# One more head pair of the first layer masked inside VectorE's row maxima, and a new order of all operations of a three-layer decoder kernel

## The reference

```python
attn = einsum('bhqd,bhkd->bhqk', q, k) / sqrt(16)
attn = softmax(where(mask, attn, -inf))
z = einsum('bhqk,bhkd->bhqd', attn, v)
x = layernorm(x + z @ W_proj + b_proj)                      # layers 0 and 1
x = layernorm(x + z + einsum('bsef,bse->bsf', experts, combine))   # layer 2
```

## Time and profile before

| what | value |
|---|---|
| median of three executions | 892.4 us |
| profiled execution, its own time | 893.21 us |
| span of the profile (first to last instruction) | 891.4 us |
| mean granted TensorE clock | 0.993 of 2.4 GHz |
| PE busy | 866.1 us, 97% |
| DVE busy | 758.7 us, 85% |
| ACT busy | 585.7 us, 66% |
| POOL busy | 416.8 us, 47% |
| DMA queue q1 | 98.77 MB, 40.6% of 16 engines' span |

### The profile page before, as it was taken

The page is one execution under the profiler, slowest core; times in us unless marked ns, Lnnn a source line. Parts: engine busy times, 40 slices in busy tenths (PEclk is TensorE's granted clock), DMA queues, the critical chain, the costliest instruction groups (busy, mean ns, idle before and its releaser), DMA issues.

```text
span 891.4 us, 28532 instructions
## 1 busy us (share of the span) xinstructions
PE 866.1 (97%) x10018; PEld 746.3 (84%) x10018; DVE 758.7 (85%) x3509; ACT 585.7 (66%) x1211; POOL 416.8 (47%) x588
## 2 busy tenths in 40 slices
PE   7899999999999999999999999999999999999996
PEld 4788888888888888989888888888888888888874
DVE  4689988998988898888888988888888888888895
ACT  4688888788878787887877644444445554555533
POOL 7688887888864545354444421122222222222201
PEclk8999999999999999999999999999999999999998
DMA  5756655664545454444434222222333333323201
GB/s 183 206 158 167 178 146 156 169 176 131 165 119 144 121 147 131 115 128 113 129 98 121 79 57 60 68 67 72 85 85 85 85 85 85 85 73 84 74 25 61
DMA packets 98268, 100.58 MB, mean 113 GB/s; under 512 B 10704, under 2 KB 90704, under 8 KB 98128
## 3 DMA queue, kind: packets, MB, share of 16 engines
q1 hardware_dynamic: 98128, 98.77, 40.6%
HBM read 18.25 MB, written 4.19 MB: 25 GB/s over the span
## 4 chain that ended last, share of the span: by engine, by line
PE 78%; issue 8%; POOL 5%; ACT 4%; DVE 2%; DMA 2%; SPq 1%; ACTq 0%; POOLq 0%; DVEq 0%
PE work L512 42%; PE work L655 9%; PE max_scores L609 8%; PE scores L632 8%; PE work L664 4%; PE scores L635 3%; PE work L537 1%; ACT attn L815 1%; PE work L673 1%; POOL attn L1156 1%; DMA k_stack<-k_parts 1%; POOL k_parts L1105 1%; POOL rstd L1147 1%; POOL q_parts L1105 1%; DMA k_stack<-in_vo 1%
## 5 line engine op out<-in xcount | busy, mean ns | idle before, releaser
L815 ACT ACTIVATE attn<-scores 128x512 f32<-128x512 f32 x384 | 214.9, 600 | 124.0 <-PE scores L632 111.1
L982 DVE CUSTOM_DVE_ANT_0 max_scores<-max_scores,mask_qk 128x128 f32<-128x128 f32 x872 | 222.9, 325 | 30.3 <-PE max_scores L609 29.3
L1098 POOL TENSOR_TENSOR q_full<-q_full,q_parts 128x512 f32<-128x512 f32 x48 | 55.9, 1166 | 274.2 <-ACT q_parts L773 274.2
L609 PE MATMUL max_scores<-k_stack,q_stack 126*128 126x128 bf16 x1536 | 142.4, 220 | 2.7 <-DMA k_stack<-k_parts 1.6
L632 PE MATMUL scores<-q_stack,k_stack 128*128 128x128 bf16 x1536 | 137.1, 220 | 3.4 <-DMA q_stack<-neg_max_t 1.6
L1057 DVE SCALAR_TENSOR_TENSOR x_all<-work,combine,x_all 128x256 f32<-128x256 f32 x256 | 121.8, 481 | 18.0 <-PE work L512 13.4
L985 DVE TENSOR_REDUCE neg_max<-max_scores 128x4 f32<-128x512 f32 x166 | 111.0, 682 | 24.1 <-PE max_scores L609 16.2
L609 PEld LDWEIGHTS max_scores<-k_stack,q_stack 126*128 126x128 bf16 x1536 | 98.1, 97 | 33.0 <-issue 18.7
L982 DVE DVE_READ_ACCUMULATOR2_ANT neg_max<- 128x1 f32 x872 | 122.9, 141 | 0.0
L632 PEld LDWEIGHTS scores<-q_stack,k_stack 128*128 128x128 bf16 x1536 | 98.1, 97 | 26.4 <-ACT attn L815 8.1
L512 PE MATMUL work<-split_hi,w_hi 128*128 128x256 f32 x384 | 113.2, 295 | 3.2 <-DVE split_lo L884 3.2
(11 more groups left out here) (126 smaller groups left out, 2020.5 us busy)
## 6 DMA issues: line engine op xcount, KB each, us to landing
k_stack<-k_parts SPq DMA_DIRECT2D x288, 128.0 KB, 2.5
q_stack<-q_parts SPq DMA_DIRECT2D x288, 128.0 KB, 2.5
in_t<-in_xt SPq DMA_DIRECT2D x16, 256.0 KB, 3.0
x_all<-in_x SPq DMA_DIRECT2D x16, 256.0 KB, 3.2
in_t<-in_ct SPq DMA_DIRECT2D x16, 256.0 KB, 2.7
out<-x_all SPq DMA_DIRECT2D x16, 256.0 KB, 2.2
stage<-in_e SPq DMA_DIRECT2D x4, 512.0 KB, 4.6
stage<-in_qk SPq DMA_DIRECT2D x2, 512.0 KB, 5.0
```

Of the source, the lines that this page charges most:

```text
L609: mm = pe.matmul(dst[:, b, h2, :], head(QS, n, 2 * p + h2, b, ROWS), head(KS, n, 2 * p + h2, b, ROWS), start=(b + h2 == 0), stop=(b + h2 = ...
L815: act.activation(attn("exp", n, p)[:, :, :], SS[g % 2][:, :, :, :].rearrange("k b h q -> k (b h) q"), ACT.Exp).then_inc(probs_done, 1)
L982: ins = dve.tensor_tensor_reduce(scores, scores, MQ[l][:, :], -1.0, HUGE, ALU.add, ALU.min, NM[n % 2][:, b, h:h + 1])
L1098: pool.tensor_tensor(FULL[x][:, :, :], FULL[x][:, :, :], PART[x][:, 0, :, :], ALU.subtract).then_inc(rest_done[x], 1)
```

## The change

Pair 7 of layer 0 joins the pairs whose mask DVE adds. That concerns items 1 to 15: PE has 15 matmuls of 512 columns fewer (8453 instead of 8468 in the program), DVE has 60 add-and-reduce instructions, with their reads, in place of 15 reductions. Layer 1 had all 8 pairs in the list already.

`PERIOD`, `TIMES`, `SHIFTS`, `starts` and `base` go. In their place `ITEM_TIMES` holds a planned time for every operation of each of the 48 items, so every item has an order of its own. The times of the weight pieces and of the two bias rows are new as well. No other function changes; banks and buffers are handed out by the same rules from the new order. Line numbers after the change are 425 higher in the functions of the engines.

```diff
-MAX_DVE = ((0, 1, 2, 4, 5, 6), (0, 1, 2, 3, 4, 5, 6, 7))
+MAX_DVE = ((0, 1, 2, 4, 5, 6, 7), (0, 1, 2, 3, 4, 5, 6, 7))
...
-PERIOD = [16.65, 18.91, 28.45]
-
-TIMES = [
-    {"q": [-39.5], "qe": [-36.65], "qh": [-35.05], "qr": [-30.39], "qm": [-27.24], "ql": [-26.79], "qs": [-38.33,
...
-SHIFTS = {
...
+ITEM_TIMES = {
+    0: {"in": [-28.35], "xr": [28.72], "xh": [-3.83], "xl": [-61.07], "q": [-15.02], "qe": [-7.1], "qh": [2.19],
...
-BIAS_TIMES = [(-27.38, -57.89), (133.26, 140.23)]
...
+BIAS_TIMES = [(3.2, -5.21), (138.61, 144.42)]
...
-ORDER = sorted([(base(n) + t + SHIFTS.get(n, {}).get(kind, 0.0), kind, n, part) for n in range(NITEM)
-                for kind, times in TIMES[layer(n)].items() for part, t in enumerate(times)]
+ORDER = sorted([(t, kind, n, part) for n in range(NITEM) for kind, times in ITEM_TIMES[n].items() for part, t in enumerate(times)]
```

More of the change, by code:

```diff
@@ L60 @@
 RB_COLS = 2 * D + E
-PERIOD = [16.65, 18.91, 28.45]
-TIMES = [
[8 rows of a table removed]
-     "norm": [33.1], "causal": [3.14, 4.3, 5.5, 6.05, 7.5, 7.59, 9.11, 10.11], "va": [-16.07]},
[12 rows of a table removed]
-     -23.67, -19.94, -18.8, -15.5, -15.16, -10.78, -9.61], "max": [-23.51, -22.57, -19.37, -17.73, -14.15,
[3 rows of a table removed]
-     [-57.01], "xl": [-54.92], "gexp": [-27.59], "gtop": [-20.22], "gateT": [-18.57], "cbt": [-17.56], "bias":
[L93 to L96, removed]
@@ L109 @@
 }
 PIECES = ["qk1", "vo1", "qk2", "vg2", "e0", "e1", "e2", "e3"]
-PIECE_TIMES = [(-8.49, 40.1, 47.02), (43.97, 76.14, 80.28), (71.5, 90.0, 111.17), (112.45, 133.83, 143.74), (140.64, 174.8, 178.0), (177.55, 192.88, 213.63), (266.43, 287.47, 303.57), (323.0, 337.9, 343.55)]
-BIAS_TIMES = [(-27.38, -57.89), (133.26, 140.23)]
-def starts():
-    first = [0.0]
-    for l in range(1, NL):
-        end, gaps = first[-1] + PERIOD[l - 1] * (NSTEP - 1), [PERIOD[l - 1]]
-        for kind in TIMES[l]:
-            if kind in TIMES[l - 1]:
-                gaps.append(max(TIMES[l - 1][kind]) - min(TIMES[l][kind]) + 0.1)
-        first.append(end + max(gaps))
-    return first
@@ L132 @@
-FIRST_BASE = starts()
-def base(n):
-    l, p = divmod(n, NSTEP)
-    return FIRST_BASE[l] + p * PERIOD[l]
+PIECE_TIMES = [(45.15, 59.57, 64.45), (78.58, 94.06, 96.95), (104.81, 112.12, 121.58), (137.24, 150.69, 164.53), (164.97, 178.87, 179.5), (189.64, 196.1, 208.83), (267.09, 270.52, 284.33), (307.08, 311.22, 312.95)]
+BIAS_TIMES = [(3.2, -5.21), (138.61, 144.42)]
 def layer(n):
```

246 lines of the change are left out of this document (added), and 274 rows, old and new, of tables (ITEM_TIMES, SHIFTS, TIMES).

## The result

The changed kernel takes 909.4 us (median of 6 runs, 907.2 to 915.8) against 892.1 us (6 runs of the kernel before on the same chips): the ratio is 1.021, with a 95% interval from 1.019 to 1.023. It is slower by 17 us where 5.8 us less were forecast, and it lies outside the range. The profiled execution took 912.1 us, its span is 910.3 us (before: 893.2 and 891.4). Times of the experiments are medians of 4 to 12 executions; one execution, of `new_sp_by_ready`, took 2134.0 us where its other three took 914.0 to 915.3, the record has no cause for it, and the ratio leaves it out.

A forecast was written before the change was run, and what follows sets the result against it. PE was taken as the bound, 97% busy, with waits left in layer 0. Terms -3.3 - 4.9 + 1.5 + 0.8 - 1.4 + 1.5 = -5.8 us gave 886.6 us; forecast range 884.5 to 889.5, 8-in-10 range 881.5 to 893.

The forecast's parts named there:

- The mask on PE: Layer 0: PE loses a 0.22 us mask matmul in each of 15 items, counted whole, -3.3 us.
- the mask is not on the path: Rival, layer 0: the mask's 3.3 us returns as waits for `max`; -2.5 us, 889.9 us, chance 0.06.
- The mask on DVE: Layer 0: DVE gains 0.41 us an item, 6.2 us in 15, against 1.7 us idle an item.
- DVE as the bound of layer 0: Rival, layer 0: DVE's added 0.41 us lengthens each item; +7.1 us, 899.5 us; slower had chance 0.13.
- Fewer waits for `zt`: Layer 0: more PE work between `zT` 1 and `zt` cuts waits from 6.4 to 1.5 us, saving 4.9.
- The start: Item 0: `q` no longer covers `maxt`'s wait for the maxima; loss 0.8 us, bounds nothing to 1.4.
- The ends of the layers: Items 46 and 47: more PE work from `k` to `s1` 0 removes waits, -1.4 us, bounds 0 and 2.
- Layers 1 and 2 otherwise: Layers 1 and 2: tighter distances, such as bank reuse in layer 2, add 1.5 us, bounds nothing and 4.9.
- DVE's maxima come late next: Layer 0: DVE's maxima must come sooner and take back 0.1 us an item, +1.5 us; bounds nothing and 6.2.
- Layer 0's period: Sign to check, layer 0: the item's period falls from 14.4 to about 13.9 us.

The follow-up runs named there:

- new_sp_by_ready: The changed kernel with SP's list sorted by when each copy's data was ready in the changed kernel's trace; 915.0 us, ratio 1.025.
- mask_only: The kernel before in its old order, with pair 7 of layer 0 masked on DVE; 892.7 us, ratio 1.0003.
- old_v_late_mask: The kernel before with the mask on DVE and `v` of layer 0 moved from -18.37 to -17.7; 893.0 us, ratio 1.0011.
- order_only: The changed kernel with its new order, but pair 7 of layer 0 masked on PE as before; 907.8 us, ratio 1.019.
- the control: The kernel before without the low part of `q` and `k` and their copies from item 3 on; 890.8 us, ratio 0.9986.
- the copy that went aside: The changed kernel with low copies from item 3 on sent to an unread DRAM tensor, `s1` 0 not waiting for them; 894.5 us, ratio 1.0029.
- new_low_by_pool: The changed kernel with POOL instead of SP issuing the low copies, right behind `kl` and `ql`; 943.4 us, ratio 1.058.
- new_pe_2us_early: The changed kernel, banks chosen from profiled starts, with only PE's order taken from moving `q` and `k` up to 2 us earlier, items 3 to 31; 949.4 us, ratio 1.064.
- old_low_by_pool: The kernel before with POOL instead of SP issuing the low copies; 922.5 us, ratio 1.034.

## Why the prediction was wrong, point by point

*The mask on PE, -3.3 us.* Right as a cost: L1037 has 23 instructions against 38, and PE's own work from start to start is 3.4 us less (the 5.7 us less that the lines show, 8.8 against 14.5 us busy, count the overlap too). Counting it whole because "PE is the engine that sets the end" was wrong for layer 0 in the old order: `mask_only` gave all of it back. That was the rival "the mask is not on the path", which I gave 0.06; it came back as waits of `zt`, though, and not of `max`.

*The mask on DVE.* Its busy time rose by the 6.2 us worked out, and its idle time covered them. The rival on the slower side, DVE as the bound of layer 0, is refuted by `mask_only`: 892.7 us, where this rival asked for 5 us more than before. I had the sign of a loss at 0.12 for a mechanism that did not act.

*Fewer waits for `zt`, -4.9 us.* The waits fell by 5.3 us. But I looked at one wait and not at the one next to it. With `v` behind it instead of ahead, `zT` comes sooner after `za`; its waits rose by 3.3 us, so that the step is worth 2.0 us. `old_v_late_mask` shows the same exchange alone, -4.1 against +3.5 us.

*The start, +0.8 us.* `maxt` waited for the maxima, as worked out:

```profile
28.93 0.28 PE L1045 MATMUL work<-ident_b,neg_max_parts 128*128 128x128 bf16 x2 [1.23 <-DVE neg_max_parts L1419]
30.56 1.01 PE L1034 MATMUL max_scores<-k_stack,q_stack 126*128 126x128 bf16 x8 [1.35 <-DMA k_stack<-k_parts]
```

Beside the earlier trace rows the scores of item 0 ended about 3 us sooner. That isn't the order's: with the old start order they began at 25.4 us in the kernel before, at 22.4 in `mask_only` and at 26.0 in `old_v_late_mask`, and with the new one at 22.3 in the changed kernel and 24.3 in `order_only`. From `s1` 7 to the first `s2` it took 6.9 us instead of 5.7. What the start cost in all can't be told apart from this spread. The cost of a wait there is larger than its length: the clock was 0.62 over the four us from 29, behind these two.

*The ends of the layers, -1.4 us.* Right for the two items named. `s1` 0 of item 47 has no wait any more, where the earlier trace rows had 0.75 us:

```profile
870.33 0.40 PE L1057 MATMUL scores<-q_stack,k_stack 128*128 128x128 bf16 x4
870.56 0.39 PE L1034 MATMUL max_scores<-k_stack,q_stack 126*128 126x128 bf16 x4
```

*Layers 1 and 2 otherwise, +1.5 us with 4.9 as the upper bound.* **This is the step that failed.** Of the distances that the new order shortens I weighed those between a bank's reader and its next writer, which layer 2 bears out (apart from `s1` 0 its waits rose from 1.1 to 2.8 us). I had the other one in hand, as the ends of the layers show: from `k` to `s1` 0, with the stack copies behind it. I looked at it in items 46 and 47 alone, where it grew. In layer 1 it shrank from 13.2 to 11.7 us, with 1.3 us to spare. But the distance is only half of it: the step also put at nothing what the order does to the length of the chain. In layer 1 the low copies stand 0.8 (`k`) and 2.0 us (`q`) longer at SP, and `q`'s low part is ready 1.5 us later behind `q`, while `k`'s is ready 1.3 us sooner. The waits of `s1` 0 grew by 10.2, 9.4 and 1.1 us, in layer 0 with a further 6 us at `s1` and `maxt`, part of it at half clock. The same omission is in layer 0, where I wrote that DVE's maxima come late next; there the waits follow the landings, two of them right behind a weight load, more than the distance. SP's queue and the new times of the weight pieces aren't in the prediction at all, though SP issues twelve stack copies of 0.60 us for each item, and the order moves every one. That the wait for the last copy costs some 15 us is shown; how it splits between distance, parts, SP's queue and landing is not. Layer 0's period, said to fall from 14.4 to 13.9 us, rose: 15.5 us from item 4 to item 14, against 14.6 before.

*What is left without that step.* With the low part left out the new order should have been ahead by what the rest of the sum says (-3.3 - 4.9 + 1.5 + 0.8 + 1.5), some 4 us. It is behind by 3.0 us. The waits of `maxt`, `zT` and the other `s1` in layer 0 are 3.9, 3.1 and 3.0 us above those of the control, and layer 2's others 1.9, against 4.9 less for `zt` and 3.7 less for `s2`; `zT`'s belong to `v`, `maxt`'s in part to the start. What makes each of the rest is not shown.

## What to carry to other kernels

When an order is changed, list every chain that leaves the bound engine and comes back to it, with the time it took, and compare each with the new distance, item by item; a chain through three engines, a queue and a DMA, with 1.3 us to spare, is the first to check and not the last. Count the large loads that go out ahead of its last copy as well. A group that is to be moved closer or further is also somebody's cover: ask what waited behind it. To find what an order costs, take the wait away without moving anything, as with the copy that went aside: moving it back told little, because each move broke another fit.

## What the runs showed of the hardware

*VectorE's small cast waits until POOL's unbroken row of computations ends.* In `new_low_by_pool` POOL issues a copy in 0.53 to 0.58 us, less than most of the delay at SP that it replaces. But `nm`'s cast on DVE, in layer 0 (64 to 230 us), first in the changed kernel and then in this one:

```profile
L1418 DVE CAST neg_max_parts<-neg_max 128x32 bf16<-128x32 f32 x11 | 2.7, 247 | 0.9
```

```profile
L1423 DVE CAST neg_max_parts<-neg_max 128x32 bf16<-128x32 f32 x10 | 20.9, 2088 | 0.8
```

It went from 0.25 to 2.09 us, and up to 5.0 us. `maxt` waits for just this: 22.0 us in 16 waits. The longer ones look like this:

```profile
140.25 2.40 POOL L1587 TENSOR_SCALAR_AFFINE_SELECT attn<-attn 128x512 f32<-128x512 f32 x4
...
140.83 3.21 DVE L1423 CAST neg_max_parts<-neg_max 128x32 bf16<-128x32 f32 x1
...
142.61 1.39 POOL L1565 TENSOR_TENSOR x_all<-x_all,row_bias 128x256 f32<-128x256 f32 x2
...
143.97 0.19 POOL L1573 TENSOR_TENSOR var_eps<-mean_var,epsilon 128x2 f32<-128x2 f32 x1
```

Six POOL computations follow each other without a gap, and the cast ends 0.04 us after the last of them, with no DMA issue beside it. So it is in all 15 casts of this run that took over 0.6 us: each ends 0.04 or 0.05 us after a POOL computation, and 4 of them overlap a DMA issue at all. A cast with only an issue beside it isn't slowed:

```profile
241.92 0.53 POOL L869 DMA_DIRECT2D q_stack<-q_parts  x1 [0.30 <-POOL q_parts L1535]
...
242.01 0.18 DVE L1423 CAST neg_max_parts<-neg_max 128x32 bf16<-128x32 f32 x1
```

It isn't the issues that hold DVE, then. They take POOL's time, and its masks and sums, late by them, come in longer unbroken rows; that this is why the rows are longer is inferred. The Trainium skill ("SBUF — State Buffer", section "SBUF: two separate sides") says that VectorE and GpSimd share a port pair under an exclusive lock, which the first to start holds for its whole instruction while the other fully blocks. The trace agrees on the block, and shows it longer than one instruction: over six here, over seven in the cast of 5.0 us. Without any DMA of POOL, in `new_pe_2us_early`, the cast took 0.42 us and up to 1.1. In `old_low_by_pool` it took 0.49 instead of 0.21 us, `w_lo` on DVE 3.6 instead of 1.2 us, and the masks on POOL were late (`pv <- POOL attn`, 12.7 us in 16 waits).

*A wait of PE costs more than its length where the clock falls behind it.*

```profile
123.25 1.01 PE L1034 MATMUL max_scores<-k_stack,q_stack 126*128 126x128 bf16 x8 [3.12 <-DMA k_stack<-k_parts]
```

Behind this wait of item 7 matmul groups took 1.0 us instead of 0.6. The granted clock was 0.57 from 121 to 129 us, and PE, idle from 120.1 to 123.25 us, then worked at or near the lower of the levels of 1.2 and 2.4 GHz. By start-to-start sums that made another 2.6 us, on top of the wait's 3.2 us. The wait of 1.3 us in item 22 above, inside layer 1, changed nothing: the clock was 1.00 there.

*A copy of a stack lands 2.5 us after its issue in the median, and later beside a load or an "instruction" packet, not beside other copies.* The copies are 128 KB. In the changed kernel's trace 244 of the 576 have no load, store or packet of an instruction queue beside them: the median is 2.4 us, and one takes over 3 us, though every one of them has other copies beside it. Of the 77 that have nothing but a 16 KB packet of q8 beside them 36 take over 3 us, up to 4.35 us. Such a packet takes 1.1 us in the mean, and there are 81 in both kernels. Right behind a load of weights, in items 5 and 7, copies took 4.85 to 6.3 us. A chain's length can't be taken as a constant in a plan.
